# One transformer layer on eight cores: the V and gate projections taken apart on TensorE, and a semaphore of its own for W_K

## The reference

```python
xn = _layernorm(x, axis=-1)
# attention: linear attention with a decayed running state, 8 heads of 64
q = phi(xn @ W_Q.T); k = phi(xn @ W_K.T); v = xn @ W_V.T      # phi(u) = elu(u) + 1
S = gamma * S + outer(k_t, v_t); z = gamma * z + k_t          # for every token t
y_t = (S^T q_t) / (z . q_t + 1e-6)
gate = sigmoid(xn @ W_g_w.T + W_g_b)
attn = (y * gate) @ W_O.T
# ffn: a dense layer and a top-2-of-8 mixture of rank-4 adapters
scores = softmax(xn @ gate_w.T); weights, idx = top_k(scores, 2)
ffn = xn @ W_lin.T + b_lin + sum_k weights_k * (xn @ left[idx_k]) @ right[idx_k]
out = x + attn + ffn
```

## Time and profile before

| | us |
|---|---|
| median of 2 runs | 441.81 (440.16 and 443.45) |
| the profiled execution | 441.92 |
| its span on core 3, the slowest | 440.8 (all cores: 434.9 to 440.8) |
| TensorE matmuls busy | 313.4 (71%) |
| VectorE busy | 205.3 (47%) |
| ScalarE busy | 131.3 (30%) |
| GpSimd busy | 24.6 (6%) |

### The profile page before, as it was taken

The page is one execution under the profiler, slowest core; times in us unless marked ns, Lnnn a source line. Parts: engine busy times, 40 slices in busy tenths (PEclk is TensorE's granted clock), DMA queues, the critical chain, the costliest instruction groups (busy, mean ns, idle before and its releaser), DMA issues.

```text
span 440.8 us, 6492 instructions; the slowest of 8 cores (434.9 to 440.8 us)
## 1 busy us (share of the span) xinstructions
PE 313.4 (71%) x2066; PEld 142.6 (32%) x2066; DVE 205.3 (47%) x807; ACT 131.3 (30%) x281; POOL 24.6 (6%) x64
## 2 busy tenths in 40 slices
PE   0003975218889987479889894588989895699866
PEld 0002332103444343223344342233434343244321
DVE  5031364134564446453666254735465276464641
ACT  3654131745214234134313234230222231400000
POOL 3700001000000000300000000200000002000000
PEclk9999999559999999568999998569999996899977
DMA  6999996000330330000221100001011100010111
GB/s 179 172 249 152 160 170 101 1 0 1 97 83 15 97 95 1 0 1 1 95 97 51 46 1 2 1 1 48 1 50 48 49 2 1 0 50 1 48 49 48
DMA packets 12851, 24.96 MB, mean 57 GB/s; under 512 B 2929, under 2 KB 7153, under 8 KB 12818
## 3 DMA queue, kind: packets, MB, share of 16 engines
q0 software_dynamic: 7856, 7.49, 12.1%
q1 hardware_dynamic: 4962, 17.05, 11.8%
HBM read 23.63 MB, written 8.39 MB: 73 GB/s over the span
## 4 chain that ended last, share of the span: by engine, by line
PE 56%; DVE 12%; ACT 11%; issue 8%; DMA 7%; POOL 4%; DVEq 1%; ACTq 0%; POOLq 0%
PE pQK L780 14%; PE pQK L792 7%; PE pG L576 7%; DMA wk_sb<-wk 7%; PE pA L395 5%; PE pQK L395 5%; PE pO L572 4%; PE pV L572 3%; PE pQK L784 2%; DVE S_sb L710 2%; ACT gsig L584 2%; PE pQK L787 2%; ACT wt L517 2%; ACT scr1b L284 2%; DVE A_sb L621 1%
## 5 line engine op out<-in xcount | busy, mean ns | idle before, releaser
L780 PE MATMUL pQK<-wlin_sb,xnfm 128*128 128x512 bf16 x256 | 66.5, 407 | 0.3
L801 DVE TENSOR_TENSOR out_sb<-pQK,x_sb 128x512 f32<-128x512 f32 x32 | 22.1, 692 | 77.6 <-PE pQK L792 77.6
L576 PE MATMUL pG<-wg_sb,xnfm 128*128 128x512 bf16 x128 | 53.2, 416 | 0.0
L572 PE MATMUL pO<-wv_sb,xnfm 128*128 128x512 bf16 x64 | 29.5, 461 | 19.9 <-DVE den_r L722 19.2
L584 ACT ACTIVATE gsig<-pG 128x512 bf16<-128x512 f32 x16 | 9.6, 598 | 110.0 <-PE pG L581 99.3
L780 PEld LDWEIGHTS pQK<-wlin_sb,xnfm 128*128 128x128 bf16 x256 | 24.8, 103 | 29.6 <-issue 8.2
L792 PE MATMUL pQK<-wo_sb,ygfm 128*128 128x512 bf16 x128 | 34.0, 389 | 0.0
L572 PE MATMUL pV<-wv_sb,xnfm 128*128 128x512 bf16 x64 | 24.2, 378 | 9.7 <-DVE den_r L722 6.7
L410 ACT ACTIVATE phir<-phiw 128x512 bf16<-128x512 f32 x32 | 19.9, 630 | 36.5 <-DVE phiw L404 36.5
L621 DVE TENSOR_TENSOR A_sb<-pA,masks 128x128 bf16<-128x128 f32 x64 | 18.2, 284 | 20.6 <-PE pG L608 20.6
L743 DVE SCALAR_TENSOR_TENSOR ygtm<-gsig,den_r,pA 128x64 bf16<-128x64 bf16 x128 | 26.0, 276 | 0.5
(11 more groups left out here) (137 smaller groups left out, 468.4 us busy)
## 6 DMA issues: line engine op xcount, KB each, us to landing
x_sb<-x SPq DMA_DIRECT2D x16, 512.0 KB, 7.8
out<-out_sb SPq DMA_DIRECT2D x16, 512.0 KB, 2.8
wlin_sb<-wlin POOLq DMA_DIRECT2D x1, 2048.0 KB, 52.7
wq_sb<-wq POOLq DMA_DIRECT2D x1, 1024.0 KB, 23.5
wk_sb<-wk POOLq DMA_DIRECT2D x1, 1024.0 KB, 30.2
wv_sb<-wv POOLq DMA_DIRECT2D x1, 1024.0 KB, 35.7
wg_sb<-wg POOLq DMA_DIRECT2D x1, 1024.0 KB, 41.2
wo_sb<-wo POOLq DMA_DIRECT2D x1, 1024.0 KB, 55.4
```

Source lines behind the costliest of these rows:

```text
L572: ins = TE.matmul(pVb[:, :], xnfm[:, 1024 * k + cs * 128 : 1024 * k + cs * 128 + 128], wv_sb[:, FH * k : FH * k + FH], start=(k == 0), sto ...
L576: TE.matmul(pG[:, :], xnfm[:, 1024 * k + cs * 128 : 1024 * k + cs * 128 + 128], wg_sb[:, FH * k : FH * k + FH], start=(k == 0), stop=False)
L780: TE.matmul(pQK[bank][:, :], xnfm[:, 1024 * k + cs * 128 : 1024 * k + cs * 128 + 128], wlin_sb[:, D * k + 512 * n : D * k + 512 * n + 512] ...
L801: ins = VE.tensor_tensor(out_sb[:, cp * D + 512 * n : cp * D + 512 * n + 512], pQK[bank][:, :], x_sb[:, cx * D + 512 * n : cx * D + 512 * ...
```

## The change

Two edits. In `E_vg`, the V matmuls are no longer interleaved with the gate's: all eight V matmuls come first and wait only for what they need (x normalised, W_V, their own bank), and the waits for W_g, the bias rows and the bank `pG` stand behind them, ahead of the eight gate matmuls. In the loading of the weights, W_K gets a semaphore of its own, `k2`, which `B_proj` waits for ahead of its fifth output. Nothing is computed differently, and no instruction is added on the engines but a wait.

```diff
@@ -139,7 +139,7 @@
-    s_wg = {g: nc.alloc_semaphore(f"s_w_{g}") for g in ["qk", "v", "g", "lg", "ow"]}
+    s_wg = {g: nc.alloc_semaphore(f"s_w_{g}") for g in ["qk", "k2", "v", "g", "lg", "ow"]}
@@ -172,7 +172,7 @@
     wmap = [(gatew_sb, gatew_d, "lg"), (left_sb, left_d, "lg"),
-            (wq_sb, wq_d, "qk"), (wk_sb, wk_d, "qk"), (wv_sb, wv_d, "v"),
+            (wq_sb, wq_d, "qk"), (wk_sb, wk_d, "k2"), (wv_sb, wv_d, "v"),
@@ -388,6 +388,8 @@
         for i, (wsb, dstfm, m) in enumerate(outs):
+            if i == 4:
+                TE.wait_ge(s_wg["k2"], w_tot["k2"])
             bank = [2, 0, 1][i % 3]
@@ -560,24 +562,25 @@
         TE.wait_ge(s_wg["v"], w_tot["v"])
+        if c >= 2:
+            TE.wait_ge(s_vec.h, rec["vfree"][c % 2])
+        for k in range(KCH):
+            ins = TE.matmul(pVb[:, :],
+                            xnfm[:, 1024 * k + cs * 128 : 1024 * k + cs * 128 + 128],
+                            wv_sb[:, FH * k : FH * k + FH],
+                            start=(k == 0), stop=(k == KCH - 1))
+        rec["vv"][c] = s_pe.inc(ins)
         TE.wait_ge(s_wg["g"], w_tot["g"])
         TE.wait_ge(s_bl, 32)
-        if c >= 2:
-            TE.wait_ge(s_vec.h, rec["vfree"][c % 2])
         if c == 0:
             TE.wait_ge(s_gp.h, ini["gp"])
         TE.wait_ge(s_sca.h, rec["gfree_s"])
         TE.wait_ge(s_vec.h, rec["gfree_v"])
         for k in range(KCH):
-            ins = TE.matmul(pVb[:, :],
-                            xnfm[:, 1024 * k + cs * 128 : 1024 * k + cs * 128 + 128],
-                            wv_sb[:, FH * k : FH * k + FH],
-                            start=(k == 0), stop=(k == KCH - 1))
             TE.matmul(pG[:, :],
                       xnfm[:, 1024 * k + cs * 128 : 1024 * k + cs * 128 + 128],
                       wg_sb[:, FH * k : FH * k + FH],
                       start=(k == 0), stop=False)
-        rec["vv"][c] = s_pe.inc(ins)
```

## The result

The changed kernel took 421.12 us (median of 11 runs, 420.81 to 421.56), the kernel before 440.95 us (median of 10). The ratio is 0.9546, with a 95% interval of 0.9526 to 0.9567: 4.5% faster. The forecast was 425.7 us, so the sign and most of the size were right. It had 16.2 us of gain from 441.9 us; 19.8 us came, from 440.95 us. So 3.6 us of gain were not foreseen, and 1 us of the difference lies in the time before. The profiled execution took 421.37 us; its slowest core is now core 1.

What follows compares the result with a forecast made beforehand. TensorE bounds the kernel by standing still, mostly for the reciprocal ahead of V. 1.3 + 1.75 + 1.7 + 11.4 = 16.15 us off core 3's 440.8 gives 424.65, with 1.1 around it 425.7 us; range 420 to 433.

Steps and rivals of the forecast that it cites:

- main term: V ahead of the reciprocal's wait in eleven chunks: 8 x 1.1 + 3 x 0.88 = 11.4 us gained, bounds 5.7 and 12.8.
- The steady chunks: V starts right behind y's last matmul; 1.1 us gained in each of eight chunks, 0.88 at three block ends.
- `ytgm` would be waited for: Expected sign in the profile: a new wait ahead of the transposes of `ytgm`, 0.2 to 0.4 us each, 4 us in all.
- the scores' second half comes 0.72 us behind: Steady chunks: L757 can't start before 213.53, the scores' second half follows at 214.25; gain 1.06 us, say 1.1.
- The semaphore of W_K: Start: q begins at 42.97 in place of 44.25, no longer waiting for W_K; 1.3 us gained, bounds 0.4 and 2.8.
- V at chunk 0: V's half fits into TensorE's 3.04 us wait for the exponentials; 1.75 us gained, bounds 1.0 and 1.75.
- the second rival: TensorE's clock, whole kernel: slow stretches move, giving 431 us (chance 0.08), or on the good side 421 to 423 (0.07).
- V at chunk 1: V fits into the 14.3 us gap, the gate alone follows the reciprocal and ends 1.7 us earlier; bounds 0 and 2.5.
- Chunks 5, 9 and 13: V and gate stay behind the same wait for the routing weights as before: no gain forecast, 0 us.
- The first: Rival: gatings or sigmoid hold up the eleven chunks, which gain 0.5 us each, 5.7 in all; 431.4 us, chance 0.10.
- the fourth: Rival: V's matmuls slow VectorE's state and reciprocal, so the gate starts later in eleven chunks; 448 us, chance 0.03.
- the third: Rival: the gains at the start and chunks 0 and 1 are lost, only 11.4 us left; 430.5 us, chance 0.06.

Runs made afterwards that it cites:

- the fourth experiment: The changed kernel with chunk 1's waits for the gate's bank put back ahead of V, in that chunk alone; 424.62 us, ratio 0.9548 against the kernel before.

## Why the prediction was right, point by point

The total owes something to luck. The moved wait, its main term, came out as forecast. The two terms that failed, 2.9 us against the change at chunk 1 and 3.5 us for it at chunks 5, 9 and 13, nearly cancel.

**The steady chunks.** Right in place and cause: the wait for the reciprocal is gone, V covers it, and the order alone does nothing. The eight chunks gained 10.3 us where 8.8 were forecast, the upper bound of 1.26 us each. Right too that `ytgm` would be waited for. The size was off by 0.2 us a chunk: the step was "the scores' second half comes 0.72 us behind" the transposes, taken from a place where TensorE had a sigmoid to wait for. Without that wait it is 0.53 us (205.57 to 206.10), so the gain is 1.25 and not 1.06 (14.88 to 13.63). At that point `ytgm` and the sigmoid (205.35 + 0.60 = 205.95, and 0.14 us for the release) let L611 go at the same moment, 206.1; bringing `ytgm` forward by 1 us moved it by nothing.

**The semaphore of W_K.** The mechanism was right, the size taken from one execution's landing. In the pair of executions that the forecast was made for, q came 1.34 us earlier, as the term of 1.3 us had it; in the comparison of its own the whole gained some 4 us, and q 3.1, above the upper bound of 2.8. The waits for W_K were 2.5 us on the forecast's core and 6.9 us on another execution's slowest core; what a wait on a load costs has the spread of the load.

**V at chunk 0.** The mechanism is as forecast: the gate's bias lies 66.11 - 64.30 = 1.8 us behind the end of the wait, and not 3.5. The size was too small: 1.75 us was the upper bound, and 2.57 came on the mean. The core that I read had run V and gate at full clock; four others had run them partly at half, and with V ahead of the wait none does. That is the good side that the second rival named, V of chunk 0 keeping the clock up.

**V at chunk 1.** This step failed: "The trace has the low level end 3.10 us after the restart on core 3, inside the gate's 3.4 us, so I keep 1.7". It was +1.17 us on the mean. The gate did end 1.6 us earlier behind the restart (98.47 - 94.97 = 3.5, before 5.1), but then TensorE waited for the sigmoid, and on six of eight cores the low level stayed or came back in the output. On the two where it came back up and stayed, chunk 1 took 15.8 us, 1.65 less than the mean before: there the term is what I had put. I had cited the rule of the Trainium skill, "TensorE: Matmul & The Clock Gate", section on the clock gate, that the price of coming back is a time and not a number of matmuls, and put it aside. It had the direction: fewer matmuls behind the gap did not make the low level shorter. It did not have the size: by it the term would have been 0, not +1.17, and the low level lasted through 14.4 us of busy time on core 1. Filling the gap took 2.9 us off chunk 1. Why cores that run the same program part in this way, 15.8 to 20.1 us, no run shows.

**Chunks 5, 9 and 13.** I had put nothing there, since V and gate stand behind the same wait as before. On core 1 before the change:

```profile
191.70 0.59 PE L537 MATMUL pT<-ident_s,wt 128*32 128x128 bf16 x4 [2.57 <-ACT wt L517]
...
197.25 0.39 PE L581 MATMUL pG<-wgb_hl,ones 2*128 2x512 bf16 x1
...
206.87 0.32 PE L670 MATMUL pO<-vtm,ktm_sb 128*64 128x65 bf16 x8
```

```profile
191.70:195.00 3.30, 3.12 (x11) 1.21 (x12) 2.65 (x12) 0.73 (x4) 0.00 (x0) 0.50 0.00 0
195.00:206.90 11.90, 10.44 (x58) 4.24 (x58) 3.73 (x12) 5.69 (x8) 0.00 (x0) 1.00 0.01 1
```

and after it:

```profile
186.69 0.38 PE L539 MATMUL pT<-ident_s,wt 128*32 128x128 bf16 x4 [1.76 <-ACT wt L519]
...
190.58 0.39 PE L584 MATMUL pG<-wgb_hl,ones 2*128 2x512 bf16 x1
...
200.19 0.32 PE L673 MATMUL pO<-vtm,ktm_sb 128*64 128x65 bf16 x8
```

```profile
186.70:200.20 13.50, 12.04 (x67) 5.03 (x67) 6.29 (x24) 6.41 (x12) 0.00 (x0) 1.00 0.01 1
```

From the transposes to the gate's bias 5.55 us before and 3.89 after; from the bias to the next chunk's state product 9.62 and 9.61. The whole difference lies in V and gate, and in their clock: 0.50 for the first 3.3 us before, 1.00 after. That is shown. Before, the level had come back ahead of them, at 188.2, and fell again behind the 2.57 us of idleness, just as they began:

```profile
188.20:191.60 3.40, 0.93 (x5) 0.19 (x2) 2.40 (x15) 1.69 (x16) 0.65 (x3) 1.00 0.01 2
```

After, it was low up to 185.5, through C_rest's eight, and then stayed up. On the mean chunk 5 is shorter in kernels with the moved wait (16.94, 18.04, 17.93, 17.49, 16.94, 18.06 in six of them) than in those without it (18.84, 18.49, 18.41). For chunk 5 the fourth experiment shows that it hangs on the waits of chunk 1: with these put back it takes 17.8 to 18.1 us on every core, as on six of eight before (17.9 to 18.3), and the case of 16.4 us is gone. So the 1.9 us that chunk 5 gained belong with the 1.2 us that chunk 1 lost, 0.7 us gained by both together, where I had 1.7. Chunk 9's 1.2 us is another thing: before, three cores took 21.2 to 21.3 us and five 17.9 to 18.1, after, all eight 17.7 to 18.1; the slow case is rarer with the moved wait (none or one of eight cores in each of six executions, two or three in each of the three without it). Why that is so, and what carries chunk 1's state to chunk 5, is not settled.

**The rivals.** The first (half the steady gain) and the fourth (VectorE slowed by V's matmuls) did not come about: the eight gatings take 1.62 us as before. Nor did the third: the start gained 3.9 us. The second did in part, on both sides at once: 2.9 us against the change at chunk 1, 3.5 for it at chunks 5, 9 and 13, and 0.8 for it at chunk 0.

## What to carry to other kernels

Put each wait ahead of the first instruction that needs it, and let independent work stand ahead of it: here one moved wait gave 1.25 us in each steady chunk, and a semaphore shared by two loads cost whatever the second was late by. When such work is moved out from behind a long gap, ask what TensorE will run right after the gap and at which clock. The same V matmuls, ahead of a gap, gained 6 us in one place, where the gap nearly closed, and nothing for the whole in another, where by my reading it stayed and less stood behind it; look at the slowest core, not at the mean. And look at the whole before paying for one stretch: what the waits put back won at chunk 1 by the clock, chunk 5 lost again.

## What the hardware showed that I had not expected

- After 11.3 us of stillness TensorE ran 14.4 us of matmuls at the level of 1.2 GHz on core 1, in a stretch that was broken by a wait for the sigmoid, where before the change 3.10 us had been enough on core 3. On two other cores of the same execution the level came back at 98.7 and 99.4 us, about at the end of the gate and its bias. With the gap filled by 40 repeated matmuls one core of eight ran the whole stretch at 2.4 GHz, and the mean was 2.9 us shorter.
- Chunk 5, some 90 us behind chunk 1, took 16.4 us on 24 of 32 cores with V ahead at chunk 1, and 17.8 us or more on all 32 with chunk 1's waits ahead of V. One pair of these kernels differs in chunk 1's waits alone.
- The same load, W_K by the queue that converts it, let q begin between 43.4 and 45.8 us in one execution and at 48.4 us on a core of another.
- From the end of the eight gatings on VectorE to TensorE's transposes it takes 0.36 us, with TensorE idle or nearly so; from the reciprocal to V it had taken 0.14 us.
